# Quarters of the second feed-forward product between projections in the quantised layer, an earlier last inverse, fewer filler products, and masked scores made in pairs

## The reference

```
L0: attention over heads inside each token, layer norm, relu feed-forward, layer norm
L1: q,k,v = 8-bit fake quantisation of h@w;  w = fakequant(softmax(q k^T/4));  x += (w v)@wo + bo
    once with itself, once with the context; then x += (a * gelu(g))@W2 + b2
L2: x = ln(x + attn(x, x, mask1)); x = ln(x + attn(x, ctx, mask2)); x = ln(x + relu(x@W1+b1)@W2+b2)
L3: x += attn(ln(x), ctx); x += attn(ln(x), ln(x), mask3); x += gelu(ln(x)@W1+b1)@W2+b2
```

## Time and profile before

| | |
|---|---|
| three runs | 1986.86, 1988.7, 1989.36 us |
| profiled execution, its time | 1985.87 us |
| its span | 1984.2 us |
| mean granted TensorE clock | 0.984 |
| PE, DVE, ACT, POOL busy | 92%, 64%, 52%, 46% |

### The profile page before, as it was taken

How to read it: one execution, slowest core, us unless ns; L and a number is a source line. 1 busy time by engine, 2 the same in 40 slices (tenths; PEclk the granted TensorE clock), 3 DMA queues, 4 the chain that set the end, 5 groups by cost and what they waited for, 6 DMA issues and landing times.

```text
span 1984.2 us, 35897 instructions
## 1 busy us (share of the span) xinstructions
PE 1822.8 (92%) x13057; PEld 1396.5 (70%) x13057; DVE 1270.0 (64%) x2286; ACT 1037.5 (52%) x3078; POOL 906.9 (46%) x1209
## 2 busy tenths in 40 slices
PE   4998889899999999999999999999999999999997
PEld 4887767677777777777767677676676776766766
DVE  5899996765675575574574756756647547365471
ACT  2222224565565475475465655655545656555662
POOL 4466555564474463472353534644434333333340
PEclk8999999899999999999999999999999999999999
DMA  8200000002000000000002000000000000000000
GB/s 236 85 11 6 11 6 6 1 7 91 1 7 6 1 7 6 1 7 7 1 7 91 1 7 6 7 7 1 7 6 1 12 1 7 22 7 1 12 1 11
DMA packets 31077, 35.73 MB, mean 18 GB/s; under 512 B 3164, under 2 KB 29752, under 8 KB 30520
## 3 DMA queue, kind: packets, MB, share of 16 engines
q1 hardware_dynamic: 30904, 33.44, 5.4%
HBM read 31.34 MB, written 2.10 MB: 17 GB/s over the span
## 4 chain that ended last, share of the span: by engine, by line
PE 63%; DVE 20%; ACT 10%; issue 6%; POOL 1%; DMA 0%; SPq 0%; DVEq 0%; ACTq 0%; POOLq 0%
PE ps L596 33%; PE ps L816 6%; PE ps L746 6%; PE ps L861 4%; PE ps L827 4%; PE ps L793 3%; ACT work L996 3%; ACT work L1003 3%; DVE work L1196 3%; PE ps L768 3%; DVE xn L1050 2%; DVE rowmax L1200 2%; PE ps L609 2%; ACT hT L910 2%; DVE O L1166 1%
## 5 line engine op out<-in xcount | busy, mean ns | idle before, releaser
L596 PE MATMUL ps<-hT,w_slot 128*128 128x256 f32 x1696 | 399.6, 388 | 20.6 <-ACT hT L910 16.1
L1325 POOL TENSOR_TENSOR work<-KT,own_head 128x512 f32<-128x512 f32 x256 | 262.4, 1047 | 284.9 <-PE ps L816 179.5
L596 PEld LDWEIGHTS ps<-hT,w_slot 128*128 128x128 f32 x1696 | 315.8, 191 | 77.6 <-ACT hT L910 21.9
L1003 ACT ACTIVATE work<-work,rowmax 128x128 f32<-128x128 f32 x768 | 244.9, 392 | 168.0 <-DVE rowmax L1200 167.2
L996 ACT ACTIVATE work<-ps,rowmax,score_scale 128x128 f32<-128x128 f32 x512 | 227.0, 470 | 141.7 <-DVE rowmax L1204 140.6
L827 PEld LDWEIGHTS ps<-ident,work 128*128 128x128 f32 x1536 | 183.9, 141 | 143.8 <-issue 74.7
L816 PE MATMUL ps<-work,QT 128*128 128x512 f32 x512 | 266.5, 605 | 9.9 <-POOL work L1325 4.9
L1401 POOL TENSOR_SCALAR work<-work,winv 128x128 f32<-128x128 f32 x512 | 185.9, 383 | 144.4 <-DVE winv L1216 142.2
L827 PE MATMUL ps<-ident,work 128*128 128x128 f32 x1536 | 233.4, 275 | 19.1 <-ACT work L1003 17.0
L1239 DVE RECIPROCAL O<-ps 128x128 f32<-128x128 f32 x128 | 122.2, 954 | 174.5 <-PE ps L861 173.8
L989 ACT ACTIVATE work<-ps 128x512 f32<-128x512 f32 x256 | 150.6, 595 | 91.6 <-PE ps L827 91.4
(11 more groups left out here) (134 smaller groups left out, 3252.1 us busy)
## 6 DMA issues: line engine op xcount, KB each, us to landing
ctx_in<-in_ctx SPq DMA_DIRECT2D x32, 256.0 KB, 2.8
w_slot<-in_L_xattn_W SPq DMA_DIRECT2D x2, 1024.0 KB, 6.3
w_slot<-in_L_xattn_ff_w SPq DMA_DIRECT2D x1, 2048.0 KB, 11.5
w_slot<-in_L_xattn_ffn_w SPq DMA_DIRECT2D x2, 1024.0 KB, 9.5
w_slot<-in_L_xattn_w SPq DMA_DIRECT2D x2, 1024.0 KB, 9.5
out<-x_all SPq DMA_DIRECT2D x8, 256.0 KB, 2.1
x_all<-in_x SPq DMA_DIRECT2D x1, 1536.0 KB, 11.6
pad<-in_mask_Bx1x1xS_fk SPq DMA_DIRECT2D x1, 1024.0 KB, 5.4
```

The costliest lines, as they stand in the source:

```text
L596: mm = pe.matmul(dst, lhsT(k), rhs(k), start=(k == 0 and not onto), stop=(k == chunks - 1 and not more))
L1003: ex = act.activation(prob[i % NPF][:, tok(h)], src[:, tok(h)], ACT.Exp, bias=shifts[:, at:at + 1])
L1325: pool.tensor_tensor(KB[u % NK].rearrange("p (h k) -> p h k", h=HU), keys, own_head[:, e:HC:2].unsqueeze(2).broadcast_to([P, HU, S]), ALU. ...
```

## The change

1. For a seam inside layer 1 (six of them: three group changes, two streams), `join` sets tin to spot 11, k 12, q 13, v and keys 14, and cuts y2 into quarters at spots 11, 12, 13, 14. All three projections use bank 7, one after the other: q waits until k has been quantised, v until q has. The sum of y2 moves into the next mix's slot 0.
2. The inverse of the last pair of units (`inverses(3)`) is emitted ahead of the pieces of step 8, not behind them, in all 16 quantised mixes.
3. `WARM_TURNS` loses unit 3: three filler products fewer in each of the 16 quantised mixes.
4. In the 24 masked mixes `scores` makes two units at once, at even steps. Each key buffer holds the keys for two units in its two halves of partitions (new mask own_four), so GpSimd spreads four times for a mix, not eight. TensorE makes four products of 64 partitions by 256 columns for the two units; the pair waits until all units before it have been masked. The heads are in another order, which `values_pair` undoes.
5. The wait for V moves from `scores(1)` to the start of step 1.

```diff
+    if layer == 1 and after == 1:
+        at.update({"tin": y2, "k": y2 + 1, "q": y2 + 2, "v": y2 + 3, "keys": y2 + 3})
...
+        pieces += [(y2 + part, end, f"y2{part}") + last[second][2:] for part in range(Y2)]
+        return pieces, [(0, tail, piece, arg, n) for piece, _, arg, n in last[second + 1:]]
...
-        WARM_TURNS = {0: 2, 1: 3, 2: 3, 3: 3}
+        WARM_TURNS = {0: 2, 1: 3, 2: 3}
...
+                    between = layer == 1 and g > 0 and piece in ("q", "v") and n["att"] == 0
...
+                        elif between:
+                            pe.wait_ge(q["k_ready"], C * (use("att", layer, g, 0) + 1))
...
-                        pe.wait_ge(q["k_ready"], C * (use("att", layer, g, n["att"]) + 1))
+                        pe.wait_ge(q["q_ready" if between else "k_ready"], C * (use("att", layer, g, n["att"]) + 1))
...
+                    if u:
+                        pe.wait_ge(s["masked"], U * masked_phase(layer, g, mix, st) + u)
+                    else:
+                        pe.wait_ge(s["exp_ready"], U * ap)
+                    for part in range(2):
+                        cols = slice(part * US // 2, (part + 1) * US // 2)
+                        for e in range(2):
+                            half = slice(e * (P // 2), (e + 1) * (P // 2))
+                            mm = pe.matmul(bank(e)[:, cols], QT[st][half, m, tok(j)], KB[u // 2][half, cols], start=True, stop=True)
+                    mm.then_inc(s["scores_ps"], 2)
...
-                    if i < U:
+                    if i < U and not (paired and i % 2):
                         scores(i)
...
-                    if quant and 0 <= i - SUM_LAG < U and (i - SUM_LAG) % 2:
+                    if quant and 0 <= i - SUM_LAG < U - 1 and (i - SUM_LAG) % 2:
                         inverses((i - SUM_LAG) // 2)
...
+                def ahead_of_pieces(i):
+                    if quant and i == U:
+                        inverses(U // 2 - 1)
+                return step, ahead_of_pieces
...
+                behind = max(u - 6, u // 2 + 1 - NK) if layer == NL - 1 else u - 6
+                pool.wait_ge(s["scores_ps"], U * ap + behind)
+                pool.tensor_tensor(KB[u // 2].rearrange("p (h k) -> p h k", h=HU), keys,
+                                   own_four[:, :].unsqueeze(2).broadcast_to([P, HU, S]), ALU.mult).then_inc(s["KB_ready"], 2)
```

More of the change, by code:

```diff
@@ L162, in join @@
     pieces = [(at.get(piece, y2 + spot - tin), start, piece, arg, n) for piece, spot, arg, n in first]
+    if layer == 1 and after == 1:
+        at.update({"tin": y2, "k": y2 + 1, "q": y2 + 2, "v": y2 + 3, "keys": y2 + 3})
+        pieces = [(at.get(piece, y2 + spot - tin), start, piece, arg, n) for piece, spot, arg, n in first]
+        second = [piece for piece, _, _, _ in last].index("y2")
+        pieces += [(spot, end, piece, arg, n) for piece, spot, arg, n in last[:second]]
+        pieces += [(y2 + part, end, f"y2{part}") + last[second][2:] for part in range(Y2)]
+        return pieces, [(0, tail, piece, arg, n) for piece, _, arg, n in last[second + 1:]]
     after_y2 = [piece for piece, _, _, _ in last].index("y2") + 2
@@ L187, with together @@
 AFTER = ("norm", "scale")
-def together(mix, steps, pieces, late):
+def together(mix, steps, pieces, late, first=None):
     chain = max(p[0] for p in pieces) + 1
@@ L198, in together @@
             mix(step_at[i])
+        if i in step_at and first:
+            first(step_at[i])
         for spot, emit, piece, arg, n in pieces:
@@ L425, in attend @@
                 kind, arg, n = PLAN[layer][2 * mix + 1]
-                together(emit_mix(kind, layer, g, st, arg, n, mix), STEPS_OF[kind], pieces, late)
+                made = emit_mix(kind, layer, g, st, arg, n, mix)
+                step, first = made if type(made) is tuple else (made, None)
+                together(step, STEPS_OF[kind], pieces, late, first)
             def ending(layer, g, after, st):
@@ L644, in emit @@
                         for m in range(C):
-                            mm = product((other if swapped else one)[:, m * T:(m + 1) * T], lambda k: w[arg["w"] % "q"][:, k, m * P:(m + 1) * P],
+                            mm = product((other if swapped or between else one)[:, m * T:(m + 1) * T], lambda k: w[arg["w"] % "q"][:, k, m * P:(m + 1) * P],
                                          lambda k: source[:, k, :], C)
@@ L786, in emit_mix @@
                 pp = None if quant else phase("plain", layer, g, mix, st)
+                paired = not quant and "mask" in arg
                 lag = ATT_LAG[quant]
@@ L865, in step @@
                 def step(i):
-                    if i < U:
+                    if i == 1:
+                        pe.wait_ge(q["v_ready"], G * (use("att", layer, g, n["att"]) + 1))
+                    if i < U and not (paired and i % 2):
                         scores(i)
@@ L1074, in emit @@
                         att = use("att", layer, g, n["att"])
+                        between = g > 0 and n["att"] == 0
                         d = 4 * arg["quant"] + "qkv".index(piece)
@@ L1081, in emit @@
                         else:
-                            dst, scratch, b = (QTb[st], QT[st], other if swapped else one) if piece == "q" else (KTb[st], KT[st], one if swapped else other)
+                            dst, scratch, b = (QTb[st], QT[st], other if swapped or between else one) if piece == "q" else (KTb[st], KT[st], one if swapped else other)
                             quantise(dst.rearrange("p c t -> p (c t)"), scratch.rearrange("p c t -> p (c t)"), b, d, at,
@@ L1335, in emit @@
                         for u in range(KEYS_AHEAD):
-                            if "quant" not in arg or u % 2 == 0:
+                            if ("quant" not in arg and "mask" not in arg) or u % 2 == 0:
                                 spread(layer, g, st, arg, n, u)
@@ L1407, in step @@
                     u = i + KEYS_AHEAD - 1
-                    if i > 0 and u < U and (not quant or u % 2 == 0):
+                    if i > 0 and u < U and (not (quant or "mask" in arg) or u % 2 == 0):
                         spread(layer, g, st, arg, n, u)
```

31 lines of the change are left out of this document (17 added, 14 removed).

## The result

The changed kernel takes 1958.7 us (four runs, 1957.0 to 1961.1) where the kernel before took 1988.3 on the same chip: a ratio of 0.9853, 95% interval 0.9835 to 0.9870, so 26 to 33 us less. The forecast was 1953, and 1958.7 lies inside its range of 1933 to 1974. The direction was as forecast; 6 of the 36 us did not come. The profiled execution has a span of 1958.1 us against 1984.2.

The account below looks back on a forecast made before the run. It took TensorE, busy 92% of the span, as the bound, with VectorE right behind in masked mixes. Terms 16 + 0 + 10.7 + 9 = 35.7 us off the median 1988.7 gave 1953 us; range 1933 to 1974.

Parts of the forecast that it names:

- The seam: Six seams of layer 1: quarters of y2 between projections gain 1.7 us each, clock 1.4 behind four; 16 us, bounds 8 and 20.
- tin-to-projection: Sign at layer 1's seams: from the tin to the output projection 14.6 us instead of 16.5.
- The inverse: Last inverse of quantised mixes made earlier: 0 us, bounds -5 and +5 (small wait of `turn` gone, or v 0.3 late).
- The fillers: Unit 3's fillers dropped in 16 quantised mixes: 0.67 us each, 10.7 us in all, bounds 0 and 10.7.
- No wait takes their place: At unit 3's turn in quantised mixes: GpSimd has weighed unit 3 by 527.93, so removing fillers leaves no new wait.
- The pairs: Masked scores of two units at once: 1.07 us a pair; 9 us gained, 6 in layer 2 and 3 in layer 3.
- the shorter xn: In masked mixes, VectorE's two xn operations, 1.24 us beside GpSimd's spreads, come nearer their undisturbed 0.8 with four spreads fewer.
- VectorE without a gap: In the masked mix walked, VectorE works without a gap from 1123.54 to 1139.68; TensorE's saving there gains 0.
- the scores' saving gets through: Rival, masked scores: TensorE's saving of 0.65 of 1.72 us reaches the end, 34 us instead of 9, time 1928; chance 0.13.
- Staggered halves: Rival, masked pairs: staggered halves or more bubbles, 0.21 us more a pair, felt at two pairs a mix; 1963, chance 0.12.
- The clock rival: Rival, quantised mixes: without fillers the clock drops once a mix, 1.4 us each, 22 in all; 1975, chance 0.04.
- The side-by-side rival: Rival, masked pairs: row halves don't run side by side, 1.93 us a pair; 2005, slower, chance 0.07.

Follow-up runs that it names:

- the light kernels: The kernel before without the division by the row sums in the masked mixes: 1978.1 us; the same with masked scores in pairs: 1957.1 us.
- the second order: The kernel after with a masked pair's products reordered, both of the upper 64 rows first, then both of the lower: 1957.9 us, ratio 0.9863.

## Why the prediction was right, and where its sizes were off

- **The seam, 16 us forecast, 13.9 measured alone.** Right in its mechanism, down to tin-to-projection. The terms: 1.3 us a seam, not 1.7, since tin to first row maximum shrank from 15.87 to 14.55; 1.3 for each clock fall, not 1.4. Four of six seams had such a fall, and none has one now. That it was four is a matter of the execution: the other four traces without a change in the order of layer 1 have three or four, and not behind the same seams.
- **The inverse, 0.** Right alone. Together with edit 3 it carries 2.2 of what is booked there (8 x 0.28), and neither of the prediction's two reasons for a change ("a small wait of `turn` gone, or v 0.3 late") was the cause; it was where V's quantising falls in GpSimd's spreads.
- **The fillers, 10.7 forecast, 2.4 measured alone by the ruler (8 x 0.3; the run times say 3 less to 1 more), about 4.6 with edit 2's help (8 x 0.58).** This is the term that failed. "No wait takes their place" was read from GpSimd's weighing of unit 3; what takes it in eight of sixteen mixes is ScalarE's unbroken work up to the gelu, the table load in it, four units later. The row 526.26 to 529.51 stood in the chain 15 times, but what is in the chain is worth its own length only if nothing runs level with it.
- **The pairs, 9 forecast, 9 measured.** Pair 1.06 us for 1.07; VectorE's wait, the shorter xn and the idle time of TensorE ahead of L844 came as walked. That the sum is right to the microsecond is in part luck: layer 2 gave 8.5 for 6, layer 3 0.5 for 3, and the two misses cancel. Layer 3 was scaled from layer 2 without walking it; there TensorE waits 2.16 us for VectorE ahead of the last pair (1619.65), and then the clock falls to 0.50 for 3.4 us, 1.1 us in each of three passes. The reason given for the small gain, VectorE without a gap, holds for part of it: with 76 us off VectorE the pairs give 21, but taking them off alone gives only 9.
- **Sum.** 13 (six seams at 1.3 and four falls at 1.3) + 4.6 + 9 = 26.6 of 35.7. The run times say 26 to 33, the spans 26.1.

The rivals: that the scores' saving gets through fell (9, not 34), and the light kernels show in part what holds it. Staggered halves, one record's 0.21 us more, fell at 1.06 us a pair. The Trainium skill, page "TensorE: Matmul & The Clock Gate", section Part 3, says that matmuls start and end in program order; in both orders of the products here the records start two abreast, while the records of one half alone start one at a time. In the second order the first two products are on the same half, so two abreast isn't that order, if the compiler kept it. Taken strictly, the rule would make the pair five steps of 0.216 us and the switch, 1.28 us, an estimate; measured is 1.06. The clock rival was put in the wrong place: from 400 us on no fall of layer 1 lies in a mix away from a seam, with the fillers or without, and the new falls came in layer 3 with the waits of pairs; they are gone with fillers in that wait, and gone without the pairs. The side-by-side rival is refuted by four records taking as long as eight.

No kernel tried here that does the whole work is shown to beat the one after.

## What to carry to other kernels

Before work is priced because it stands in the chain, look for the second chain that ends within its length: here ScalarE's exponentials and table load, four units on, took half of it. Where two engines are both full, expect little from lightening one: pairs and a lighter VectorE gave 9 each alone and 30 together, some of it by the clock. Look also at a third engine: halving GpSimd's spreads with TensorE's work as it was gave 9.5. And when a change gives TensorE a new wait, ask for the clock: the wait of 2.16 us here had a stretch at the lower level, 1.2 GHz, behind it in three passes of four of its trace.

## What was not expected of the hardware

- A VectorE operation on 128x512 float32, from SBUF to SBUF, took 0.43, 0.83, 0.88 or 1.13 us in the same place of the program: 0.43 by itself, else to 0.28 us after the end of the GpSimd operation that ran when it started.
- The score products of 64 rows by 256 columns took 1.06 us to the next work whether one half of the rows was in use (four records) or both (eight), and whichever order the program gave them.
- The granted clock falls in stretches of 3.4 us at 0.50, some twice as long. Which seams it falls behind is not set by the code: 514, 667, 770 and 821 us in the trace before; 514, 616, 668 and 821 with half the spreads in the masked mixes, and 616, 667 and 821 without the masked divisions, all three with the same code for layer 1. So a difference of one or two us between two profiles of layer 1 can come from that alone.
